# A gated cross-attention block on one core: quantiser inputs read from PSUM, the softmax split moved between engines, and a rescaling by 256 folded into constants

## The reference

```python
ln_out = _ln(_layernorm(x), ln_w, ln_b)
def _div_clamp_fp8(x, scale):
    y = jnp.clip(x / scale, -448, 448)
    y = y.astype(jnp.bfloat16).astype(jnp.float32)
    return _fp8_roundtrip(y)
q, qx, k, v = (einsum(_div_clamp_fp8(ln_out, s) * s, w) * w_scale for the four kinds)
# q, qx, k and the key of the context are layer-normed per head of 128
core = softmax(q k^T / sqrt(128)) v        # 8 groups of 2 heads, 256 keys
xout = softmax(qx kx^T / sqrt(128)) vx     # 64 keys of the context
catq = _div_clamp_fp8(concat(core, xout), proj_smooth)
x = x + tanh(g_xattn) * (catq wproj^T) * (proj_in_scale * proj_w_scale)
x = x + tanh(g_ffn) * moe_ffn(_layernorm(x))     # 8 experts, best two, and a shared one
```

## Time and profile before

| what | value |
|---|---|
| median of three runs | 1059.95 us |
| the profiled execution | 1060.97 us |
| its span (first to last instruction) | 1059.2 us |
| busy: PE, DVE, ACT, POOL | 942.8, 837.0, 756.5, 718.0 us |
| mean granted TensorE clock | 0.968 |

### The profile page before, as it was taken

One profiled execution on the slowest core, in us unless ns is written; L12 is line 12 of the kernel. 1 busy time (PEld: TensorE's weight loads), 2 busy tenths in 40 slices (PEclk: granted clock), 3 DMA queues, 4 the chain that ended last, 5 costly groups with the idle time before them and its releaser, 6 DMA issues.

```text
span 1059.2 us, 21165 instructions
## 1 busy us (share of the span) xinstructions
PE 942.8 (89%) x6752; PEld 668.4 (63%) x6752; DVE 837.0 (79%) x1715; ACT 756.5 (71%) x2378; POOL 718.0 (68%) x533
## 2 busy tenths in 40 slices
PE   1376899999899899999989999998975999999998
PEld 0264576677687677667767767776742555555554
DVE  8898989989999999999999999999965653333332
ACT  3476898899899899889989989998963432222222
POOL 4597888799789878979979887897842322232222
PEclk9787899999999999999999999999987999999999
DMA  9324142242232323323223223232345100000000
GB/s 250 104 70 127 26 76 50 51 76 50 53 71 53 71 50 63 61 50 72 52 50 74 50 50 74 50 70 54 69 92 139 57 1 20 1 20 0 20 0 20
DMA packets 183266, 63.13 MB, mean 60 GB/s; under 512 B 167248, under 2 KB 180912, under 8 KB 183232
## 3 DMA queue, kind: packets, MB, share of 16 engines
q1 hardware_dynamic: 179120, 60.62, 26.8%
q0 software_dynamic: 4112, 2.10, 1.4%
HBM read 20.76 MB, written 2.10 MB: 22 GB/s over the span
## 4 chain that ended last, share of the span: by engine, by line
PE 41%; issue 22%; POOL 16%; DVE 15%; DMA 1%; ACT 1%; SPq 1%; POOLq 0%; DVEq 0%; ACTq 0%
PE S L422 7%; POOL rstd L1342 5%; POOL pT L1454 4%; PE A L325 4%; PE A L326 4%; PE S L410 4%; DVE zq L926 4%; PE T L393 3%; POOL raw L1404 3%; PE VB L317 2%; DVE qT L1037 2%; PE JB L452 2%; PE VB L319 2%; PE VB L318 2%; DVE stage L974 2%
## 5 line engine op out<-in xcount | busy, mean ns | idle before, releaser
L1342 POOL TENSOR_TENSOR rstd<-var,mhalf 128x8 f32<-128x8 f32 (+1 forms) x128 | 201.9, 1606 | 101.8 <-DVE var L1051 100.9
L325 PE MATMUL A<-w_hi,xq 128*128 128x256 f16 (+1 forms) x1024 | 189.4, 251 | 31.5 <-DVE v_lo L1025 20.6
L1454 POOL TENSOR_TENSOR pT<-zq,pT 128x512 f16<-128x512 f32 (+1 forms) x56 | 65.3, 1166 | 183.3 <-ACT pT L856 175.3
L326 PE MATMUL A<-w_lo,xq 128*128 128x256 f16 (+1 forms) x1024 | 189.4, 251 | 0.0
L422 PE MATMUL S<-kT,qT 128*128 128x256 f32 x512 | 142.5, 402 | 8.9 <-ACT kT L723 6.0
L861 ACT ACTIVATE qT<-A 128x512 f32<-128x512 f32 (+1 forms) x56 | 33.4, 596 | 152.8 <-PE A L319 152.8
L735 ACT ACTIVATE prob<-S,nmx 128x256 f32<-128x256 f32 x256 | 119.4, 476 | 17.6 <-DVE nmx L1009 17.2
L325 PEld LDWEIGHTS A<-w_hi,xq 128*128 128x128 f16 x1024 | 102.4, 100 | 42.1 <-issue 25.8
L1404 POOL TENSOR_TENSOR raw<-raw,rstd 128x1024 f32<-128x1024 f32 x64 | 126.7, 1980 | 0.0
L1009 DVE TENSOR_REDUCE nmx<-S 128x2 f32<-128x512 f32 (+1 forms) x192 | 114.5, 596 | 15.2 <-PE S L422 11.8
L1037 DVE TENSOR_SCALAR qT<-T,qmap 128x512 f32<-128x512 f32 x128 | 102.1, 806 | 29.8 <-PE T L393 28.9
(11 more groups left out here) (183 smaller groups left out, 2681.0 us busy)
## 6 DMA issues: line engine op xcount, KB each, us to landing
stage<-wallT SPq DMA_DIRECT2D x8, 1024.0 KB, 5.1
wp<-wpT POOLq DMA_DIRECT2D x1, 2048.0 KB, 30.6
out<-v_lo SPq DMA_DIRECT2D x8, 256.0 KB, 2.2
xs<-x SPq DMA_DIRECT2D x1, 1792.0 KB, 20.7
pT<-psrc SPq DMA_TRANSPOSE x64, 4.9
sq<-w2s SPq DMA_DIRECT2D x7, 128.0 KB, 3.0
sq<-w1T SPq DMA_DIRECT2D x3, 256.0 KB, 3.4
sq<-w3T SPq DMA_DIRECT2D x3, 256.0 KB, 3.3
```

Source lines behind the costliest of these rows:

```text
L325: nc.tensor.matmul(o, l, w_hi[:, c, col:col + n], start=(c == 0), stop=False)
L326: last = nc.tensor.matmul(o, l, w_lo[:, c, col:col + n], start=False, stop=(c == HC - 1))
L1342: return nc.gpsimd.tensor_tensor(dst, src, mhalf[:, 0:n], ALU.pow)
L1454: nc.gpsimd.tensor_tensor(a_lo[0:n, j % 3, :], act_b[0:n, j % 2, :], a_hi[0:n, j % 3, :], ALU.subtract).then_inc(f_alo, 1)
```

## The change

- The quotients of the front are made from bank A1 directly, with ln_w/scale and ln_b/scale (`ysc`, `ybi`, both divided by 256, made once at the start) as scale and bias: kinds 0 and 1 by ACT (four activations in g = 2), kinds 2 and 3 by DVE (four passes at the end of g = 2, after ACT's). The tile lnT goes away. PE's next use of A1 waits for both. The clip moves from g = 4 to g = 3. The rounding is done in g = 7 in two passes that write `xq`.
- POOL's `normalise_p` writes the f16 high half of P into psrc (it now waits for the DMA that transposed this buffer two steps ago); 1/sum is multiplied by PSCALE first (`scale_sums`). ACT's `high_p` goes away. DVE's `low_p` makes the low half in four passes with 1/sum as scalar.
- No multiplication by 256 after either rounding; the factor goes into the weight scales' row, vscale and gates. `sums` moves ahead of `low_v`.

```diff
-            def front_ln(fb):
+            def front_scale(fb):
                 done(act, fr_T, fb)
-                for c in range(HC):
-                    last = nc.scalar.activation(lnT[:, c, :], A1[:, c * S:(c + 1) * S], ACT.Identity,
-                                                bias=vec[:, C_LNB + c:C_LNB + c + 1], scale=vec[:, C_LNW + c:C_LNW + c + 1])
-                last.then_inc(fr_ln, 1)
+                done(act, fr_xk, fb - 1)
+                for k in range(2):
+                    for c in range(HC):
+                        m = k * HC + c
+                        last = nc.scalar.activation(yq[:, k, c, :], A1[:, c * S:(c + 1) * S], ACT.Identity,
+                                                    bias=ybi[:, m:m + 1], scale=ysc[:, m:m + 1])
+                last.then_inc(fr_ya, 1)
...
                         if g == FRONT_G + 1:
-                            done(pe, fr_ln, b + 1)
+                            done(pe, fr_ya, b + 1); done(pe, fr_yd, b + 1)
...
-                if live(n0 - 3): high_p(n0 - 3, par(3), 3)
...
-            def front_scale(fb, kinds):
+            def front_scale(fb):
-                if kinds[0] == 0:
-                    done(dve, fr_ln, fb)
-                for k in kinds:
+                done(dve, fr_ya, fb)
+                for k in range(2, 4):
                     for c in range(HC):
-                        last = nc.vector.tensor_scalar(yq[:, k, c, :], lnT[:, c, :], rins[:, k * 2 + c:k * 2 + c + 1], None,
-                                                       ALU.mult)
+                        m = k * HC + c
+                        last = nc.vector.tensor_scalar(yq[:, k, c, :], A1[:, c * S:(c + 1) * S], ysc[:, m:m + 1], ybi[:, m:m + 1],
+                                                       ALU.mult, ALU.add)
+                last.then_inc(fr_yd, 1)
...
-            def front_round(fb):
-                dve.wait_ge(fr_q, fb * 2 + 1)
-                bits = zq[:, :, :, :].bitcast(U16)
-                nc.vector.tensor_scalar(bits, bits, RNE7, RNE7, ALU.add, ALU.subtract).then_inc(fr_q, 1)
-            def front_xq(fb, k):
-                dve.wait_ge(fr_q, fb * 2 + 2)
-                nc.vector.tensor_scalar(xq[:, k:k + 2, :, :], zq[:, k:k + 2, :, :], 1.0 / Q8, None, ALU.mult
-                                        ).then_inc((fr_xq, fr_xk)[k // 2], 1)
+            def front_round(fb, k):
+                done(dve, fr_q, fb)
+                nc.vector.tensor_scalar(xq[:, k:k + 2, :, :].bitcast(U16), zq[:, k:k + 2, :, :].bitcast(U16), RNE7, RNE7,
+                                        ALU.add, ALU.subtract).then_inc((fr_xq, fr_xk)[k // 2], 1)
...
                 def low_p(n, p):
-                    done(dve, a_ph, n)
-                    nc.vector.scalar_tensor_tensor(psrc[:, p, PSELF:2 * PSELF], prob[:, p, :, :, :].rearrange("p k j s -> p (k j s)"),
-                                                   PSCALE, psrc[:, p, 0:PSELF], ALU.mult, ALU.subtract).then_inc(d_pl, 1)
+                    done(dve, g_norm, n)
+                    hi, lo = (psrc[:, p, k * PSELF:(k + 1) * PSELF].rearrange("p (k j s) -> p k j s", j=PJ, s=P) for k in range(2))
+                    for j in range(PJ):
+                        last = nc.vector.scalar_tensor_tensor(lo[:, :, j, :], prob[:, p, :, j, :], rl[:, p, j:j + 1], hi[:, :, j, :],
+                                                              ALU.mult, ALU.subtract)
+                    last.then_inc(d_pl, 1)
...
+                def scale_sums(n, p):
+                    done(dve, d_rc, n)
+                    nc.vector.tensor_scalar(rl[:, p, :], rl[:, p, :], PSCALE, None, ALU.mult).then_inc(d_rl, 1)
...
-                def widen_out(n, p):
-                    done(dve, d_rnd, n)
-                    nc.vector.tensor_scalar(cq[:, p, :, :], cq[:, p, :, :], 1.0 / Q8, None, ALU.mult).then_inc(d_cq, 1)
...
                 if live(n0 - 3): low_p(n0 - 3, par(3))
-                if live(n0 - 5): widen_out(n0 - 5, par(5))
                 if live(n0 - 3): low_px(n0 - 3, par(3))
...
                 if live(n0 - 1): maxima(n0 - 1, par(1), 0)
+                if live(n0 - 2): sums(n0 - 2, par(2))
                 if live(n0): low_v(n0)
+                if live(n0 - 2): scale_sums(n0 - 2, par(2))
                 if live(n0 - 1): maxima(n0 - 1, par(1), 1)
-                if live(n0 - 2): sums(n0 - 2, par(2))
...
-                    if g == FRONT_G: front_scale(b + 1, (0, 1))
-                    if g == FRONT_G + 1: front_scale(b + 1, (2, 3))
-                    if g == FRONT_G + 2: front_clip(b + 1)
-                    if g == FRONT_G + 4: front_round(b + 1)
+                    if g == FRONT_G: front_scale(b + 1)
+                    if g == FRONT_G + 1: front_clip(b + 1)
                     if g == G - 1:
                         done(dve, mm_kv, n0)
-                        front_xq(b + 1, 2)
+                        front_round(b + 1, 2)
...
                 def normalise_p(n, p):
                     done(pool, d_rl, n)
+                    if live(n - 2):
+                        pool.wait_ge(ld_pT[p], (b * (G // 2) + (g - 2) // 2) * 16)
                     nc.gpsimd.tensor_tensor(
-                        prob[:, p, :, :, :], prob[:, p, :, :, :],
+                        psrc[:, p, 0:PSELF].rearrange("p (k j s) -> p k j s", j=PJ, s=P), prob[:, p, :, :, :],
                         rl[:, p, 0:PJ].rearrange("p (o j i) -> p o j i", o=1, i=1).to_broadcast([P, ST, PJ, P]), ALU.mult
                         ).then_inc(g_norm, 1)
```

More of the change, by code:

```diff
@@ L87, in build @@
         rins = sb("rins", [P, 8], F32)
+        ysc = sb("ysc", [P, 8], F32)
+        ybi = sb("ybi", [P, 8], F32)
         rsm = sb("rsm", [P, 2 * NH], F32)
@@ L179, in build @@
         ctx_hi_done = sem("ctx_hi_done")
-        fr_st, fr_var, fr_rs, fr_sub, fr_z1, fr_z2, fr_T, fr_ln, fr_y, fr_q, fr_xq, fr_xk = (sem("fr_" + n) for n in (
-            "st", "var", "rs", "sub", "z1", "z2", "T", "ln", "y", "q", "xq", "xk"))
+        fr_st, fr_var, fr_rs, fr_sub, fr_z1, fr_z2, fr_T, fr_ya, fr_yd, fr_q, fr_xq, fr_xk = (sem("fr_" + n) for n in (
+            "st", "var", "rs", "sub", "z1", "z2", "T", "ya", "yd", "q", "xq", "xk"))
         ctx_lo_done = sem("ctx_lo_done")
+        fr_map = sem("fr_map")
         ta_st, ta_var, ta_rs, ta_sub, ta_z, ta_T, ta_hi, ta_lo = (sem("ta_" + n) for n in ("st", "var", "rs", "sub", "z", "T", "hi", "lo"))
@@ L189, in build @@
         ld_pT = [sem("ld_pT0"), sem("ld_pT1")]
[L190 to L193, removed]
+        a_q0, a_sq1, a_q1, a_sqk, a_v, a_vxh, a_x, a_kT, a_e0, a_e1, a_ex, a_phx, a_core, a_xo = (
+            sem("a_" + n) for n in "q0 sq1 q1 sqk v vxh x kT e0 e1 ex phx core xo".split())
+        d_v, d_vx, d_ssq, d_ss, d_varq, d_var, d_qT, d_qxT, d_m0, d_m1, d_mx, d_rc, d_rl, d_pl, d_plx, d_clip, d_cq, d_x1 = (
+            sem("d_" + n) for n in "v vx ssq ss varq var qT qxT m0 m1 mx rc rl pl plx clip cq x1".split())
         g_rstdq, g_uq, g_rstd, g_u, g_normx, g_norm = (sem("g_" + n) for n in "rstdq uq rstd u normx norm".split())
@@ L753, in high_px @@
                     turned(n, p, lag)
[L754 to L760, removed]
+                    nc.scalar.activation(pair(p)[:, :, 0, :], probx[:, p, :, :], ACT.Copy).then_inc(a_phx, 1)
                 def scale_out(n, p, k, og):
@@ L821, in tick @@
                 if g == FRONT_G:
-                    front_ln(b + 1)
+                    front_scale(b + 1)
                 if g == TAIL_G and live(b - 1, B):
@@ L832, in _ @@
             scale(0)
-            front_ln(0)
+            act.wait_ge(fr_map, 1)
+            front_scale(0)
             high(0)
@@ L1098, in tick @@
                         sums(n0 - 2, par(2))
+                        scale_sums(n0 - 2, par(2))
                         done(dve, mm_kT, STEPS - 1)
@@ L1103, in tick @@
                         sums(n0 - 1, par(1))
+                        scale_sums(n0 - 1, par(1))
                     if g == 1:
@@ L1189, in _ @@
             own(nc.vector.reciprocal(epsw[:, :], wsrow[:, :]))
+            nc.vector.tensor_scalar(rins[:, :], rins[:, :], Q8, None, ALU.mult)
+            own(nc.vector.memset(hold_cell[:, 0:1], 0.0))
+            for m, c in ((ysc, C_LNW), (ybi, C_LNB)):
+                last = nc.vector.tensor_tensor(m[:, :].rearrange("p (k c) -> p k c", c=HC),
+                                               rins[:, :].rearrange("p (k c) -> p k c", c=HC),
+                                               vec[:, c:c + HC].rearrange("p (o c) -> p o c", o=1).to_broadcast([P, 4, HC]), ALU.mult)
+            last.then_inc(fr_map, 1)
             nc.vector.tensor_scalar(epsw[:, :], epsw[:, :], EPS, None, ALU.mult)
-            nc.vector.tensor_scalar(rins[:, :], rins[:, :], Q8, None, ALU.mult)
             nc.vector.tensor_scalar(rsm[:, :], rsm[:, :], Q8 / (PSCALE * VSCALE), None, ALU.mult)
-            nc.vector.tensor_scalar(vscale[:, :], scl[:, S_WV:S_WV + 1], VSCALE, None, ALU.mult)
```

(7 more changed lines are left out.)

25 lines of the change are left out of this document (9 added, 16 removed).

## The result

The changed kernel takes 1067.9 us (median of 5 runs, 1066.07 to 1070.54) against 1059.73 for the kernel before on the same chip: ratio 1.0083, 95% interval 1.0059 to 1.0107. It is slower, by 0.8%. The forecast was 1026.5, with 1036 as its upper end. The profiled execution has a span of 1064.3 us.

A forecast was written before the change was run, and what follows sets the result against it. PE bounds plain steps (10.23 us); DVE, its passes waiting for POOL, bounds two long steps a batch. Gains of 30.6 + 0 (start) + 1.1 + 1.8 = 33.5 give 1027.5 from 1060.97, 1026.5 against the median; range 1017 to 1036.

The forecast's parts named there:

- Part 2: Making P: POOL's f16 product no change, at most 0.14 more; low_p's four passes +0.2, at most +0.5; scale_sums 0.1 to 0.2.
- the first batch: First batch: DVE's savings vanish behind POOL's w_lo; only the earlier 1/sum stays, a gain of 1.1 us (0 to 5).
- (d): Rival, DVE's low_p: its four passes lose the SBUF port to POOL, so the kernel gets slower, 1120 us; chance 0.03.
- Part 1: Front's quotients from PSUM no longer wait for POOL: three steps gain 1.8, 2.3 and 0.26, 4.4 us a batch, 30.6 total.
- the drain: End of the program: no high_p and no widening, low_p longer twice, a gain of 1.8 us.

The follow-up runs named there:

- P as before: Changed kernel with POOL's product in place in f32, ACT's high_p, one low_p pass and no scale_sums, quotients from PSUM kept: 1030.4 us.
- before with four passes: Kernel before the change, with only low_p in four passes of 256 columns, times the constant PSCALE, instead of one of 1024: 1078.4 us, ratio 1.0187.

## Why the prediction was wrong

**The step that failed** is the last sentence of Part 2, "scale_sums adds 0.1 to 0.2 behind the maxima". It was mis-sized in two ways. It took the price of a free eight-column instruction (0.15 to 0.17 in the five free ones); measured are 0.84 on average, and 44 us of the total with all that hangs on it. And it named a place that the diff does not give it: maxima(1) stands behind the scaling, and ACT's exponentials behind that. At the place that I had in mind it costs some 6 us. I had the evidence in hand: the earlier trace rows shows twelve columns held for 3.87 us, and the earlier trace rows has L1404 starting 0.7 behind low_px. I used them for low_p and for the first batch, not for the one instruction that the change puts inside this product in nearly every step. No rival named it either; (d) had the right mechanism on the wrong instruction, and its bound of 1120 is no nearer than my range.

The Trainium skill (SBUF — State Buffer, "Who interferes with whom") states that a tensor_scalar can enter a mode that takes both port pairs, and then blocks until a running GpSimd instruction is over. The trace agrees: 59 of 59 overlapping ones end with POOL's product. I had cited this section for instructions of two SBUF inputs alone.

**Part 1** was right. The passes from PSUM never waited: 528 to 544 ns for all 36, of which 32 start while POOL has an instruction running, and four take 1.90 (1.8 forecast) against 4.31 in the earlier trace rows. The step with the front takes 11.53 without the scaling, 11.5 forecast. The next two are at 10.22 to 10.30. These three steps gain 4.4 us a batch, 4.4 forecast. Six batches without the scaling are 32.0 us shorter than before, 26.2 forecast (six sevenths of 30.6). Nearly all of the other 5.8 comes from three further steps of each batch (11.16 to 10.77, 10.52 to 10.22, 10.82 to 10.57 on average), which I had at nothing; which part of the change brings them is not shown. With P as before the six are 21.2 shorter, but the 10.8 between the two is the one long step of that kernel (12.3 against 10.2) and no measure of Part 2.

**Part 2, low_p.** Four take 1.66 in place of 1.21: +0.45, the far end of "at most +0.5". With a constant factor they take 1.42, so 0.06 of each is the factor read per partition. POOL's f16 product takes 1.89, no change, as forecast. Its wait for the flip never shows (4.1 us from issue to landing).

**The first batch** was forecast at a gain of 1.1 and loses 1.5 without the scaling, 8.1 with it. There rival (d) is real: in three steps one low_p pass waits for POOL (2.1 us). My argument against it was that L1404 starts after the run. In the full batches it does (1.95 us or more behind the start of a run of 1.66); in these three steps it starts 0.1 to 0.5 ahead of the run, as it already did in before.

**The whole.** Without the scaling: +1.5, -32.0, and -7.1 behind step 57, against -1.1, -26.2 and -6.2 forecast (one batch and the drain): 1023.9, inside the range. The forecast was of that kernel, and it is in part luck that it came so near: the batches and the drain gave 6.7 more than forecast, the first batch 2.6 less.

## What to carry to other kernels

Price a small DVE instruction by what POOL runs at that moment, not by its columns: look up in the timeline which product is open there, and how the two engines release each other, because a phase set by semaphores repeats in every step. Ask of the instruction's form whether any row shows it waiting, and put a form that waits where the product has ended, or behind what others wait for. A saving ahead of such a wait is worth nothing until the wait is gone, as the kernel with one low_p pass shows.

## What the runs showed of the hardware

- A tensor_scalar of 8 (or 2) fp32 columns from SBUF to SBUF is held for the rest of POOL's running 128x1024 product: up to 1.63 us for 0.15 us of work. A reciprocal of the same tile never is (182 to 203 ns in 64, 59 of them started inside the product).
- Whether POOL gets in between four consecutive passes with two SBUF operands went with the form of their factor. In three steps of the first batch POOL's product starts 0.10, 0.10 and 0.50 us ahead of the run, in both kernels alike. With the constant factor all passes of the run took 405 to 426 ns and the product waited (3.61, 3.61, 4.34). With the factor from SBUF the product took 1.94, 1.93 and 2.33, and the first pass 2.11 or 2.12. The two kernels differ in more than the factor, so that it is the cause is not shown.
- A 128x256 pass with two SBUF operands (low_px) that starts 0.24 or 0.25 us behind the start of POOL's 128x1024 product takes 2.12 us in place of 0.41, six times in before with four passes.
